# Tokens queued per expert: two full one-expert tiles of 512 rows a batch in place of all four experts for every token

## What is computed

```python
x = x + attention(layernorm(x))
xf = layernorm(x).reshape(-1, 128)                      # 8192 tokens
logits = xf @ wr + br                                   # 4 experts
topk_vals, topk_idx = top_k(logits, 2)
gates = softmax(topk_vals)
h = gelu(einsum('nd,edh->enh', xf, w1) + b1)            # 4 x 8192 x 512
y = einsum('enh,ehd->end', h, w2) + b2                  # 4 x 8192 x 128
c = gelu(b1) @ w2 + b2                                  # per expert, c_sum over experts
out = x + einsum('nk,nkd->nd', gates, y[chosen] - c[chosen] + c_sum)
```

## Time and profile before

| | |
|---|---|
| median of 3 runs | 979.45 us (973.37 to 982.94) |
| span of the profiled execution | 979.1 us |
| PE, matmuls | 909.5 us busy, 93% |
| PEld, weight loads | 602.9 us, 62% |
| DVE | 555.5 us, 57% |
| ACT | 459.5 us, 47% |
| POOL | 182.8 us, 19% |
| DMA | 99.5 MB, mean 102 GB/s; SP's queue 30.9% of the 16 engines, POOL's 4.0% |
| mean granted clock of PE | 0.959 of 2.4 GHz |

### The profile page before, as it was taken

How to read it: one execution, slowest core, us unless ns; L and a number is a source line. 1 busy time by engine, 2 the same in 40 slices (tenths; PEclk the granted TensorE clock), 3 DMA queues, 4 the chain that set the end, 5 groups by cost and what they waited for, 6 DMA issues and landing times.

```text
span 979.1 us, 24109 instructions
## 1 busy us (share of the span) xinstructions
PE 909.5 (93%) x9572; PEld 602.9 (62%) x9572; DVE 555.5 (57%) x1552; ACT 459.5 (47%) x740; POOL 182.8 (19%) x183
## 2 busy tenths in 40 slices
PE   2794999999999999999999999999999999999995
PEld 1463676665766666666666666666666666666662
DVE  7533636667474756657474755747475665736321
ACT  1321364463736355463736455373635446373640
POOL 5601011212102121211112121220212121210211
PEclk9965779999999999999999999999999999999998
DMA  7413060533515152442516143352615243350110
GB/s 206 126 49 83 13 203 25 144 105 99 151 55 171 32 162 83 127 122 76 174 27 189 40 143 102 105 146 63 165 29 166 79 138 102 82 157 2 56 54 14
DMA packets 96021, 99.50 MB, mean 102 GB/s; under 512 B 8968, under 2 KB 82704, under 8 KB 95888
## 3 DMA queue, kind: packets, MB, share of 16 engines
q1 hardware_dynamic: 93168, 85.19, 30.9%
q0 software_dynamic: 2544, 12.58, 4.0%
q10 hardware_dynamic: 192, 0.13, 0.1%
HBM read 48.20 MB, written 28.71 MB: 79 GB/s over the span
## 4 chain that ended last, share of the span: by engine, by line
PE 66%; DVE 17%; issue 8%; ACT 5%; SPq 1%; DMA 1%; POOL 1%; DVEq 0%; POOLq 0%; ACTq 0%
PE y_ps L400 15%; PE s_ps L309 8%; PE o_ps L343 5%; PE s_ps L332 5%; PE s_ps L258 5%; PE s_ps L260 5%; DVE rmax L649 5%; PE s_ps L259 5%; ACT hid L936 4%; PE v_ps L318 2%; PE a_ps L373 2%; PE o_ps L350 2%; PE a_ps L267 2%; DVE nmax L658 2%; SPq L1107 1%
## 5 line engine op out<-in xcount | busy, mean ns | idle before, releaser
L400 PE MATMUL y_ps<-hid,w2s 128*128 128x512 f32 x480 | 243.9, 609 | 0.0
L900 ACT ACTIVATE prob<-s_ps 128x1024 f32<-128x1024 f32 x128 | 131.1, 1025 | 222.1 <-PE s_ps L332 222.1
L649 DVE TRANSPOSE_TENSOR_REDUCE rmax<-s_ps 128x16 bf16<-128x512 f32 x256 | 167.3, 691 | 65.8 <-PE s_ps L309 65.5
L936 ACT ACTIVATE hid<-s_ps,b1s 128x512 f32<-128x512 f32 x256 | 171.4, 688 | 36.8 <-PE s_ps L260 36.5
L309 PE MATMUL s_ps<-qdiag,kv 64*128 64x512 f32 x768 | 138.4, 467 | 14.9 <-DMA kv<-kv_chosen 7.5
L309 PEld LDWEIGHTS s_ps<-qdiag,kv 64*128 64x128 f32 x768 | 86.8, 257 | 43.8 <-issue 14.7
L258 PE MATMUL s_ps<-xnhi,w1hi 128*128 128x512 f32 x256 | 112.2, 438 | 1.5
L658 DVE TENSOR_REDUCE nmax<-v_ps 16x64 bf16<-16x256 bf16 x128 | 52.4, 409 | 107.4 <-PE v_ps L325 106.8
L1036 POOL TENSOR_TENSOR yT<-yT,gate_cols 128x512 f32<-128x512 f32 x48 | 61.7, 1285 | 271.4 <-DVE gate_cols L745 271.0
L893 ACT COPY vaug<-v_ps 128x128 f32<-128x128 f32 x128 | 34.0, 266 | 156.6 <-PE v_ps L318 155.8
L332 PEld LDWEIGHTS s_ps<-nmax,hone 16*128 16x128 bf16 x2048 | 69.0, 95 | 54.9 <-issue 27.5
(11 more groups left out here) (146 smaller groups left out, 1095.7 us busy)
## 6 DMA issues: line engine op xcount, KB each, us to landing
gate_cols<-gates SPq DMA_DIRECT2D x64, 256.0 KB, 5.2
kv_table<-stage SPq DMA_DIRECT2D x16, 768.0 KB, 3.9
kv<-stage SPq DMA_DIRECT2D x16, 768.0 KB, 6.2
kv_chosen<-selected SPq DMA_DIRECT2D x15, 768.0 KB, 5.3
kv<-kv_chosen SPq DMA_DIRECT2D x15, 768.0 KB, 4.9
qdiag<-qpair SPq DMA_DIRECT2D x504, 16.0 KB
xs<-in_x SPq DMA_DIRECT2D x16, 256.0 KB, 4.4
out_x<-x SPq DMA_DIRECT2D x16, 256.0 KB, 4.7
```

The costliest lines, as they stand in the source:

```text
L400: ins = pe.matmul(dst[:], w2s[:, n, :], hid[:, n, :], start=(c == 0), stop=(c == C - 1))
L649: v.tensor_reduce(rmax[m % 2][:, half * 8:(half + 1) * 8, :], s_ps[m % 2][:, half * N:(half + 1) * N].rearrange("p (a c) -> p a c", c=32), ...
L900: act.activation(prob[m % 2][:].rearrange("p h s -> p (h s)"), s_ps[m % 2][:], ACT.Exp, scale=SCALE).then_inc(exped, 1)
L936: act.activation(hid[:, k, :], up_ps[up_bank(k)], ACT.Gelu, bias=b1s[:, k:k + 1]).then_inc(gelued, 1)
```

## The change

The four experts are no longer applied to every token. Each token's normalised row (128 floats, with its four gates and its number: 136 floats) is written twice into a queue in device memory, once for each expert that it chose, and the experts work on tiles of 512 consecutive rows of one expert's queue. The steps are these.

- `c_prefix` on PE, `c_address` on DVE: five small bf16 matmuls count the tokens of each expert ahead of each token, eight small operations turn that into addresses. `scatter` on POOL: eight indirect DMAs a batch, 128 rows of 544 bytes each.
- `c_pick` on DVE: 15 small operations choose the tiles from the full ones of the four queues. Beginning with batch 3 two tiles are processed per batch, 27 in all until batch 15 and 8 after it (`FLUSH`), 35 in place of 64.
- `take_w`, `take_x` on POOL: an indirect DMA gathers the weights of a tile (128 rows of 6160 bytes), another its rows (128 rows of 2176 bytes).
- `x_columns` on PE turns the rows, `x_high` on ACT and `x_low` on DVE split them, `c_gate_of` on DVE picks the gates. `c_up` is the three matmuls as before, four times per tile. `c_down` now has the hidden values as the stationary operand: 16 matmuls of 128 columns per tile, one group of four per block of attention, and its result has tokens as rows.
- `c_out` on ACT multiplies by the gate. `add_rows` on POOL: four indirect DMAs per tile add the rows to the output in device memory. `c_bias` on PE and `c_biased` on DVE add the constant part of the experts per batch, so x2 is stored without waiting for the experts.
- The stores and broadcasts of gates, `c_gated`, `c_sum`, `c_turn`, `c_add` and the split of the normalised rows are gone.
- SP copies empty rows over the queue (16 copies of 1.1 MB in batches 0 to 2) and writes w1, w2 and b1 of each expert to one table (about 3.9 MB, in batch 1).

Not changed are the eight blocks of attention, the block choice and its way through memory.

```diff
@@ constants
-UP_SPREAD = 3 * C + 1
+UP_SPREAD = C + 1
+LAG = 3
+STEADY = 2 * (B - LAG) + 1
+FLUSH = 8
+TILES = STEADY + FLUSH
+RING = 4
@@ def tensor(pe), the loop over batches and blocks
-                    if b >= 2 and not edge:
-                        c_down(b - 2, 2 * m)
+                    if b > LAG and not edge:
+                        c_down(first_tile(b - 1) + m // T, m % T)
...
+                    if b >= LAG and m == M - 1:
+                        x_columns(first_tile(b))
                 weighted(b, M - 1)
                 o_project(b, T - 2)
                 for k in range(UPS):
-                    if b >= 1:
-                        c_up(b - 1, k)
+                    if b >= LAG:
+                        c_up(first_tile(b) + k // C, k % C)
                     if k == 1:
                         o_rows(b, T - 1)
+                        if b >= LAG:
+                            x_columns(first_tile(b) + 1)
@@ def pool(g)
+            def take_x(tile):
...
+                if tile >= RING:
+                    g.wait_ge(added, 16 * T * (tile - RING + 1))
+                g.indirect_dma_start(
+                    out=xt[:, slot, :], out_offset=None, in_=quads,
+                    in_offset=bass.IndirectOffsetOnAxis(ap=x_index[which][:, j:j + 1], axis=0)).then_inc(x_got[slot], 16)
+            def add_rows(tile, i):
...
+                    if tile >= 1:
+                        g.wait_ge(added, 16 * T * tile)
+                g.wait_ge(*copied_out(tile, i))
+                g.indirect_dma_start(
...
+                    in_=y_rows[:, n % (2 * T), :], in_offset=None, compute_op=ALU.add).then_inc(added, 16)
@@ def pool(g), the loop
+                    if b > LAG and m >= 1:
+                        add_rows(first_tile(b - 1) + (m - 1) // T, (m - 1) % T)
                     if b >= 1 and m == 5:
-                        c_split(b - 1)
+                        scatter(b - 1)
...
+                if b > LAG:
+                    add_rows(first_tile(b - 1) + 1, T - 1)
+                for tile in tiles_at(b):
+                    take_w(tile)
+                for tile in tiles_at(b):
+                    take_x(tile)
                 inverse(b, mv2, veps2, rstd2, mean2_done, rstd2_done)
```

## The result

The kernel after takes 1527.8 us (1526.5 to 1532.1), the one before 979.5 us beside it: a ratio of 1.562, 95% interval 1.556 to 1.567. It is slower, as forecast, but by 56% and not by 19%; 1528 us lie far outside the range of 1060 to 1290.

What follows compares the result with a forecast made beforehand. It took the chain through DVE, PE and ACT and the chosen blocks' way as the bound, not PE's work. Start 205, batch 3 62, 11 periods of 65 and end 182 gave 1164 us; forecast 1165, range 1060 to 1290.

Steps and rivals of the forecast that it cites:

- step 1: POOL's scatter: starts when c_address is done, 23.5 us after a batch's zero; eight DMAs of 1.25 bring it to 33.7.
- step 4: PE's clock: with c_down at half clock the first blocks are PE's own; 1.5 us per batch (none to 8).
- 63.7 (+1.5 for the clock): Length of a batch, zero to zero: 63.7 us, 8 more than before; with the clock's 1.5 a period of 65.
- I take this for all kinds.: POOL's indirect DMAs: all kinds start 1.25 us apart; bounds 0.95 and, for the adding kind, 2 us.
- They share one queue... 48.7.: Tile's gathers: first weights land at 45.0, second at 47.6, the rows 1.1 later at 48.7; PE waits some 12 us.
- Zero of batch 3 at 205.: Start: batch 3 begins at 205 us as before (206); batches 1 and 2 take 56 us each.
- Rival D: Start: the clearing chokes the queue engine, +40 us on the forecast, 1205 us; chance 0.04.
- End at about 182.: From batch 15's zero to the span's end: about 182 us, against 104 before; 215 with adds at 2 us.
- rival C: Blocks and POOL: half clock through the blocks and adds at 2 us or more, period 72, end 225, 1288 us; chance 0.14.
- The new c_down: PE's c_down with 32 records of 128 columns per tile: 3.9 us per tile, between bounds of 3.6 and 6.4.

Runs made afterwards that it cites:

- e15: The kernel after, unchanged, loaded and run a third time, without the stop: 1408.7 us, ratio 1.442 to the kernel before.
- e18: The kernel after with the add_rows as plain indirect writes that overwrite, without the stop: 1366.0 us, ratio 1.401 to the kernel before.
- e10: The kernel after without the scatter, with unread matmuls on PE in the wait for the rows and at the batch's seam: 1348.8 us, ratio 1.380.
- e1: The kernel before with the matmuls of experts 2 and 3 cut from 512 to 32 columns: 1048.8 us, ratio 1.071.
- e9: The kernel after with the queues' clearing issued behind the batch's copies for the choice, without the stop: 1404.5 us, ratio 1.433 to the kernel before.
- e14: The program of e9, unchanged, run again in another set, with the stop: 1532.5 us, ratio 1.562 to the kernel before.
- e13: The kernel after, unchanged, run a second time, with the stop: 1536.9 us, ratio 1.564 to the kernel before.
- e3: The kernel after with a batch's four tile gathers issued in block 6, ahead of the last two add_rows: 1444.6 us, ratio 1.478.

## Why the prediction was wrong

The sign and the outline of the mechanism were right: the removed matmuls gave nothing back, and a wait for the gathered rows stands in each batch. What was wrong is what that wait hangs on (step 1), what the removed matmuls did for the clock (step 4), and the sizes, all to one side; the stop was not foreseen. Over one batch, from its zero:

| | forecast | after (batch 4) | e15, no stop (batch 7) |
|---|---|---|---|
| scatter starts | 23.5 | 34.3 | 31.6 |
| row maximum 7 | 35.5 | 54.7 | 40.4 |
| choice's gather issued | 33.7 | 48.5 | 41.7 |
| first take_w | 39.6 | 61.0 | 48.7 |
| first take_x | 42.1 | 63.6 | 51.3 |
| rows there, PE goes on | 48.7 | 71.5 | 61.2 |
| next zero | 63.7 (+1.5 for the clock) | 89.1 | 79.2 |

The last column rests on these rows, of DVE (the end of c_address), ACT (c_out of block 4) and POOL, and then of PE (zero 536.89, next 616.08):

```profile
563.23 0.17 DVE L870 TENSOR_SCALAR slot_of<-slot 128x8 uint32<-128x8 f32 x1
565.43 0.37 ACT L1127 ACTIVATE y_rows<-y_ps,gsel 128x128 f32<-128x128 f32 x1
566.59 1.55 POOL L1299 DMA_INDIRECT out_x<-y_rows,xt  x1 [6.53 <-ACT gateT L1113]
568.45 1.00 POOL L1259 DMA_INDIRECT queue<-rows,slot_of  x1 [0.30 <-issue]
...
578.63 1.01 POOL L1236 DMA_INDIRECT selected<-kv_table,index  x1 [0.31 <-issue]
579.95 1.62 POOL L1299 DMA_INDIRECT out_x<-y_rows,xt  x1 [0.30 <-issue]
...
585.60 1.00 POOL L1271 DMA_INDIRECT wt<-experts,w_index  x1 [0.30 <-issue]
...
588.18 0.95 POOL L1286 DMA_INDIRECT xt<-queue,x_index  x1 [0.30 <-issue]
```

```profile
578.66 0.33 PE L453 MATMUL v_ps<-idn,att 128*128 128x128 f32 x1
598.05 1.09 PE L504 MATMUL a_ps<-idn,xt 128*128 128x128 f32 x4 [19.07 <-DMA xt<-queue,x_index]
```

Along this path the batch of e15 is 15.5 us longer than forecast: 8.1 until the scatter starts, 1.1 from the choice's gather to take_w, 3.3 in the landing of the rows, 3.0 from there to the next zero. The steps that failed:

1. **"The scatter can start when c_address is done, 23.5."** This step failed by 8 us. c_address is done at 26.5, since blocks 0 and 1 took 13.4 us in place of 10.6 (step 4). And in POOL's program an add_rows stands ahead of the scatter, which waits for the c_out of block 4, goes out at 29.7 and takes 1.9. With it 17 indirect DMAs follow each other without a pause, so POOL's queue, and no longer c_out of block 7, decides when take_w goes out: 48.7 in place of 39.6. The prediction followed what is queued behind PE's wait, and not what stands ahead of the scatter on POOL.
2. **1.25 us from start to start: "I take this for all kinds."** Right for writes and gathers (1.27), but 1.87 us for the adding kind, near the bound of 2. Four adds stand on POOL's way in each batch, one ahead of the scatter and three behind the choice's gather, 2.4 us by the 0.6 each; e18, 2.5 per batch shorter, agrees and puts the price at 43 us in all.
3. **"They share one queue... 48.7."** The landing took 9.9 us from the issue of take_x, not 6.6. The choice's store and its reading back, 768 KB each (SP at 583.68 and 590.30), lie beside the tile's gathers, where the sum let the tile have the queues alone; the DMA share in such a wait is 0.88.
4. **The clock: "I take 1.5 us per batch (none to 8)."** Row maximum 7 came 4.9 us later than forecast (6.8 in the mean of batches 4 to 14), and from the rows to the next zero it took 18.0 us in place of 15.0. e10 puts blocks 0 to 2 at 4 to 5 us; e1 shows the same kind of loss in the kernel before. That the 3.0 us are the clock's too is argued: it is 0.50 in the first 8 us behind the rows of e15, where six matmuls of c_up start 0.43 apart and not 0.23, but no run held it up there. The error was in kind: the clock was taken for a cost of the new wait alone, and the removed work for "nothing". That PE's filling work held the clock stood in no term, though rows 8 had the half clock in batch 1, whose blocks have no c_down.
5. **The stop** was in no rival. It is 22.8 - 12.5 = 10 us more until the rows are there, 9 of the period, and with its share at start and end 120 us of the kernel after.
6. **"Zero of batch 3 at 205."** 226 without the stop and 236 with it. Batch 1 lasted 69.9 in place of 56; with the clearing behind the choice's copies 63.7 in e9, but 69.7 in e14, which has the stop (72.0 in e13), so how much of it is the clearing's is left open. In e15's batch 2 the gather went out at 36.2 and the next zero came 25.9 later, against 20.4 before. Rival D had the place right and half the price.
7. **"End at about 182."** 226 and 240. Take 26 goes out 70 after the zero, not 57, as batch 15 has the same late tile; the adds cost 17; the four last add groups lie 9.7 to 9.8 apart and not 8. Some 14 us were not separated. The sum was thin as well: 98, three tiles of 9.5 and four groups of 8 make 158.5, and the 23.5 for PE's part have no term of their own.

In sum, without the stop: 21 + 8 + 11 x 15.3 + 44 = 241 us over 1164, which is e15's span of 1405. With the stop 126 more, the profiled 1530. Three slips of the sum are small: 23.5 and 8 x 1.25 make 33.5 and not 33.7, 35.5 with 2.65 and two copies of 0.27 makes 38.7 and not 38.3, and in rival C 32 records at 0.21 are 2.8 us over the 3.9 and not 3.5. Its reach to 1290 (rival C, half clock and adds of 2 us) was the nearer story: both of its halves, the half clock and dear adds, are there, but on a scatter that started late. The new c_down was well priced at the full clock: 8 records in 1.06 us, 4.2 per tile against 3.9. The wait itself is 13.7 us in batch 4 of the kernel after and 19.1 in batch 7 of e15, against 12. Where the stop makes block 7 late, PE comes late to its wait, and so the run with the stop has less of it (211 us in all against 261).

The Trainium skill (page "Trainium Kernel Development and Optimization", section "Performance Expectations") names the busy share of the weight loads as one of two good measures of the distance to the limit. The clock can't be seen in it: e1 has 63% against 62% before, and is 7% slower.

## What to carry to other kernels

A matmul that hides in a gap isn't free to remove: in e1 taking it out brought PE's clock to the half in the next stretch, and a run like e1 measures this before a rewrite, by thinning the work and looking at the time. When work goes to POOL as indirect DMAs, lay its whole queue out in time, each DMA 1.27 us and each adding one 1.87, with what stands ahead of each; here 17 in a row became the path. And run the unchanged kernel once more, in another set, before an edit far away gets the credit.

## What had not been expected of the hardware

- The granted clock fell when half of the experts' matmuls were taken out: mean 0.96 to 0.80, period 55.8 to 61.4 us.
- One program has two times, 1409 and 1528 to 1537 us. In the slower one PE, DVE and ACT start next to nothing for 8 us beside POOL's eight indirect writes, and in e3 for 7 us beside four gathers, even where the DMA share is low (0.12); in the faster one they work through the same traffic. The cause is open.
- An indirect DMA with an addition costs POOL 1.57 us of issue and 1.87 from start to start, one without 0.97 and 1.27.
